# Attention on 64x64 tiles of TensorE, with the softmax sums inverted where they lie

## What is computed

```python
q, k, v = (einsum('bnd,fd->bnf', layernorm(x), W).heads(16, 64) for W in (Wq, Wk, Wv))
sim = 50 * tanh(einsum('bhid,bhjd->bhij', q, k) / 8 / 50)      # [2, 16, 1024, 1024]
attn = softmax(where(causal, sim, -max), axis=-1)
x = x + einsum('bhij,bhjd->bhid', attn, v).merge_heads() @ Wo.T
```

## Time and profile before

| | us |
|---|---|
| median of 3 runs | 1235.56 |
| lowest, highest | 1235.16, 1241.74 |
| profiled execution: time, span | 1238.81, 1237.1 |
| TensorE busy | 1153.2 |
| VectorE busy | 848.6 |
| ScalarE busy | 718.5 |
| GpSimd busy | 523.7 |

### The profile page before, as it was taken

The page is one execution under the profiler, slowest core; times in us unless marked ns, Lnnn a source line. Parts: engine busy times, 40 slices in busy tenths (PEclk is TensorE's granted clock), DMA queues, the critical chain, the costliest instruction groups (busy, mean ns, idle before and its releaser), DMA issues. The chain is left out here.

```text
span 1237.1 us, 20696 instructions
## 1 busy us (share of the span) xinstructions
PE 1153.2 (93%) x6995; PEld 575.1 (46%) x6995; DVE 848.6 (69%) x1836; ACT 718.5 (58%) x945; POOL 523.7 (42%) x545
## 2 busy tenths in 40 slices
PE   4899999999999998879997999999999999888998
PEld 1444444444444485358983222222222223446996
DVE  6456666666666555864426899999999995485441
ACT  3587787787787715512225276767767777651221
POOL 0056656656656700337863013213312311135884
PEclk9799999999999999979999999999999999897999
DMA  4000101001001110427754431322122120223765
GB/s 126 1 7 19 25 24 35 24 24 35 24 24 35 23 33 5 171 63 189 179 120 83 84 66 44 60 54 56 49 60 51 45 53 1 78 98 100 193 171 121
DMA packets 54878, 81.98 MB, mean 66 GB/s; under 512 B 18776, under 2 KB 36572, under 8 KB 53676
## 3 DMA queue, kind: packets, MB, share of 16 engines
q1 hardware_dynamic: 42728, 70.92, 21.2%
q0 software_dynamic: 10880, 8.86, 4.9%
q10 hardware_dynamic: 1192, 1.19, 0.3%
HBM read 55.38 MB, written 11.67 MB: 54 GB/s over the span
## 5 line engine op out<-in xcount | busy, mean ns | idle before, releaser
L1866 ACT ACTIVATE at_PR<-psum 128x1024 f32<-128x1024 f32 x256 | 248.0, 1021 | 121.2 <-PE psum L2098 121.0
L1934 DVE TENSOR_REDUCE at_MX<-psum 128x1 f32<-128x512 f32 x468 | 301.0, 685 | 10.0 <-PE psum L2075 5.4
L1803 POOL TENSOR_TENSOR at_PR<-at_PR,at_FAC 128x512 f32<-128x512 f32 x64 | 81.0, 1266 | 285.8 <-ACT at_PR L1866 285.8
L486 ACT ACTIVATE PR<-psum 128x1024 f32<-128x1024 f32 x144 | 141.0, 1026 | 73.7 <-PE psum L774 61.3
L774 PE MATMUL psum<-Q,K 64*128 64x512 f32 (+3 forms) x768 | 143.6, 502 | 1.1 <-ACT PR L486 1.1
L491 ACT ACTIVATE PR<-PR 128x1024 f32<-128x1024 f32 x144 | 144.6, 1062 | 0.0
L786 PE MATMUL psum<-PR,V 128*64 128x512 f32 (+3 forms) x768 | 137.4, 489 | 0.1
L2116 PE MATMUL psum<-at_PR,at_VG 128*32 128x512 f32 x1024 | 136.2, 604 | 0.0
L2098 PE MATMUL psum<-at_QS,at_KS 122*128 122x512 bf16 x512 | 133.4, 381 | 0.4 <-ACT at_PR L1866 0.2
L463 POOL TENSOR_SCALAR_AFFINE_SELECT PR<-PR 128x256 f32<-128x256 f32 (+1 forms) x112 | 58.8, 539 | 160.3 <-ACT PR L491 159.9
L1456 PE MATMUL psum<-moe_XGT,moe_WE 128*128 128x256 f32 x512 | 125.4, 390 | 0.0
(11 more groups left out here) (256 smaller groups left out, 1706.0 us busy)
## 6 DMA issues: line engine op xcount, KB each, us to landing
moe_WE<-in_c_We SPq DMA_DIRECT2D x32, 768.0 KB
XB<-at_r_dram SPq DMA_DIRECT2D x32, 256.0 KB, 3.8
at_QS<-at_SPL SPq DMA_DIRECT2D x72, 64.0 KB
at_KS<-at_SPL SPq DMA_DIRECT2D x72, 64.0 KB
at_KS<-in_c_krows SPq DMA_DIRECT2D x8, 384.0 KB
moe_rows_dram<-XNS SPq DMA_DIRECT2D x2, 1152.0 KB, 10.7
moe_spare_dram<-moe_zeros SPq DMA_DIRECT2D x2, 1024.0 KB, 13.3
moe_sum_dram<-XB SPq DMA_DIRECT2D x2, 1024.0 KB, 3.8
```

Source lines behind the costliest of these rows:

```text
L486: act.activation(PR[u][:, :, :], S[(b + u) % 2][:, :, :], ACT.Tanh, scale=SCALE0 / CLAMP).then_inc(z.clamped, 1)
L1803: pool.tensor_tensor(pr, pr, FAC[:, 4 * (s // 2):4 * (s // 2) + 4, :], ALU.mult).then_inc(z.factored, 1)
L1866: act.activation(PR[:, gu % PRS, 2 * r:2 * r + 2, :].rearrange("p h n -> p (h n)"), g.psum[:, 2 * r * BANK:(2 * r + 2) * BANK], ACT.Exp).t ...
L1934: dve.tensor_reduce(MX[:, 4 * (2 * pair + c % 2) + I % 4, khalf:khalf + 1], bank(("max", c))[:, :], AX, ALU.max).then_inc(z.reduced, 1)
```

## The change

Every matmul of the attention's loop now uses a quarter of the array, 64 rows by 64 columns.

- `scores`: each matmul is split in two column halves `c`. With the heads' row halves that makes four.
- The query blocks stand in the order `ORDER` = 2, 3, 4, 5 | 0, 1, 6, 7, one half in each output bank. A unit's first two blocks (`near`) belong to the first bank, the others (`far`) to the second.
- `multiply`: two passes. In the first, one half of the contraction (64 rows) goes to the one bank and the other half to the other bank; in the second they swap. The second pass waits for the first (`z.halved`).
- `project` for Q, K, V and `totals`: likewise in two passes over the two banks of `J`. `totals` gives 64 equal rows for each head, in both banks: its output is already broadcast.
- `copy_totals`, `spread` and `broadcast` go. `invert` takes the reciprocal of the two banks from PSUM into RB, 128x512 each, before `scale`.
- `take` moves from ScalarE to VectorE (but for the last sequence), at `n == 1` and `n == 10` in VectorE's order.
- TensorE's scores are `AHEAD` = 4 units ahead of its products. The scores of unit n + 4 stand between the two passes of unit n.
- A sequence has five masked units instead of seven, one with four diagonal blocks.

```diff
+ORDER = [2, 3, 4, 5, 0, 1, 6, 7]
+BLOCKS = [[(0, 2), (0, 3), (0, 0), (0, 1)], [(0, 4), (0, 5), (0, 6), (0, 7)], [(1, 2), (1, 3), (1, 6), (1, 7)],
+          [(2, 2), (2, 3), (2, 6), (2, 7)], [(3, 4), (3, 5), (3, 6), (3, 7)], [(3, 3), (5, 5), (1, 1), (7, 7)],
+          [(4, 4), (4, 5), (4, 6), (4, 7)], [(1, 4), (1, 5), (5, 6), (5, 7)], [(2, 4), (2, 5), (6, 6), (6, 7)]]
+PIECES = [(runs(u[0:2], 0), runs(u[2:4], 2 * P)) for u in BLOCKS]
...
+AHEAD = 4
...
@@ VectorE
-                def copy_totals(s):
+                def take(s, b, p):
+
+                    dve.wait_ge(z.multiplied, NU * s + NU)
+                    for half in range(2):
+                        dve.tensor_copy(heads_out(p, b, half * BANK, (half + 1) * BANK), O[:, half * BANK:(half + 1) * BANK]
+                                        ).then_inc(z.taken, 1)
+
+                def invert(s):
+
                     dve.wait_ge(z.totalled, s + 1)
-                    wait(dve, z.spread, 64 * s)
-                    dve.tensor_copy(DS[:, :], J[0]).then_inc(z.copied, 1)
-
-                def invert(s):
-                    dve.wait_ge(z.spread, 64 * s + 64)
-                    dve.reciprocal(RC[:, :, :], RC[:, :, :]).then_inc(z.inverted, 1)
+                    wait(dve, z.scaled, s)
+                    for j in range(2):
+                        dve.reciprocal(RB[:, j * BANK:(j + 1) * BANK], J[j]).then_inc(z.inverted, 1)
...
                 def pair(p, more):
                     first = isinstance(p, int) and p == 0
+                    for n in range(2 * NU):
+                        add_up(dve, 2 * p + n // NU, n // NU, n % NU, 0, z.summedA)
+                        if n == 1 and not first:
+                            take(2 * p - 1, 1, p - 1)
+                        if n == 10:
+                            take(2 * p, 0, p)
+                        if n in (1, 3, 5):
+                            projected(2 * p + 1, 1, n - 1)
+                            projected(2 * p + 1, 1, n)
+                        if n in (10, 12, 14) and more:
+                            projected(2 * p + 2, 0, n - 10)
+                            projected(2 * p + 2, 0, n - 9)
+                        if n == 7 and not first:
+                            invert(2 * p - 1)
+                            scale(2 * p - 1, 1, p - 1)
+                        if n == 16:
+                            invert(2 * p)
+                            scale(2 * p, 0, p)
@@ TensorE
+                def project(s, b, side, first):
+
+                    if first and side == 0:
+                        wait(pe, z.inverted, 2 * s - 4)
+                        pe.wait_ge(z.value, 2 * s)
+                    elif first:
+                        pe.wait_ge((z.query, z.key)[side - 1], 2 * s + 2)
+                    if not first:
+                        pe.wait_ge(z.part_projected, 3 * s + side - 2)
+                    passed(s)
+                    for t in range(4 if side == 2 else 1):
+                        for x in range(2):
+                            rows = row[x if first else 1 - x]
...
+                def multiply(s, b, u, swap, first):
+
+                    if first and u == 0:
                         pe.wait_ge(z.value, 2 * s + 2)
-                    if u < 2:
-                        wait(pe, z.taken, 2 * s - 1 + u)
-                    unit_done(pe, s, u)
-                    for j, at, q, w in PIECES[u]:
+                        wait(pe, z.taken, 2 * s)
+                    if first:
+                        unit_done(pe, s, u)
+                    else:
+                        pe.wait_ge(z.halved, NU * s + u + 1)
+                    passed(s)
+                    for n in range(2):
+                        for side in range(2):
+                            rows = row[side if first != swap else 1 - side]
+                            for j, at, q, w in PIECES[u][side][n:n + 1]:
+                                for h in range(2):
+                                    mm = pe.matmul(O[row[h], q:q + w], V[rows, b, j, row[h]], PR[u][rows, h, at:at + w],
+                                                   start=(first and u == 0), stop=(not first and u == NU - 1),
+                                                   skip_group_check=True)
+                    mm.then_inc(z.halved if first else z.multiplied, 1)
+
+                def totals(s, b, value, first):
+                    if first:
+                        pe.wait_ge(z.summedA, ADDED[NU] * (s + 1))
+                        pe.wait_ge(z.summedB, ADDED[NU] * (s + 1))
+                        wait(pe, z.inverted, 2 * s)
+                        pe.wait_ge(z.value, value)
+                    else:
+                        pe.wait_ge(z.part_totalled, s + 1)
+                    passed(s)
+                    for j in range(2):
+                        rows = row[j if first else 1 - j]
                         for h in range(2):
+                            mm = pe.matmul(J[j][row[h], :], g.ones[rows, 0:DH0], ACC[b][rows, h, j * BANK:(j + 1) * BANK],
+                                           start=first, stop=not first, skip_group_check=True)
+                    mm.then_inc(z.part_totalled if first else z.totalled, 1)
 
                 def pair(p, more):
...
+                    for n in range(2 * NU if more else 2 * NU - AHEAD):
+                        turned = n == 0 or n == NU and more
+                        if turned:
+                            if n:
+                                pe.wait_ge(z.w, 16 * p + 32)
+                            project(2 * p + 1 + n // NU, 1 - n // NU, 0, True)
+                            scores(*unit(n + AHEAD))
+                        multiply(*unit(n), n % 2 == 1, True)
+                        if turned:
+                            project(2 * p + 1 + n // NU, 1 - n // NU, 0, False)
+                        else:
+                            scores(*unit(n + AHEAD))
+                        multiply(*unit(n), n % 2 == 1, False)
+                        k = n % NU
+                        if 1 <= k <= 4 and (n < NU or more):
+                            project(2 * p + 1 + n // NU, 1 - n // NU, (k + 1) // 2, k % 2 == 1)
+                        if n in (5, 6) and not begin:
+                            totals(2 * p - 1, 1, 4 * p + 4, n == 5)
+                        if n in (14, 15):
+                            totals(2 * p, 0, 4 * p + 6, n == 14)
```

More of the change, by code:

```diff
@@ L389, in add_up @@
                 unit_done(eng, s, u)
-            for k, (to, w, first, second) in enumerate(ADDS[u]):
-                into = ACC[b][:, h, to:to + w]
+            for k, (n, to, first, second) in enumerate(ADDS[u]):
+                into = split(ACC[b][:, h, :], n)[:, to, :]
                 if second is None:
@@ L504, in pair @@
                             exponent(s, u)
-                        if k == 0 and not (isinstance(p, int) and p == 0):
-                            for half in range(2):
-                                take(2 * p - 1, 1, p - 1, half)
-                        if k in (4, 5):
-                            take(2 * p, 0, p, k - 4)
                 def first_copies(first, end):
@@ L790, in totals @@
-                def totals(s, b, value):
-                    pe.wait_ge(z.summedA, ADDED[NU] * (s + 1))
-                    pe.wait_ge(z.summedB, ADDED[NU] * (s + 1))
-                    pe.wait_ge(z.value, value)
-                    for h in range(2):
-                        for j in range(2):
-                            at = (2 * h + j) * ROWS
-                            mm = pe.matmul(J[0][at:at + ROWS, :], g.ones[:, 0:ROWS], ACC[b][:, h, j * BANK:(j + 1) * BANK],
-                                           start=True, stop=True, skip_group_check=True)
-                    mm.then_inc(z.totalled, 1)
@@ L881, in _ @@
                 for k in (4, 5):
-                    project(0, 0, k)
-                scores(0, 0, 0)
-                scores(0, 0, 1)
-                pe.wait_ge(f1.next.xt, 4)
+                    project_first(k)
+                for u in range(AHEAD):
+                    scores(0, 0, u)
+                    if u == 1:
+                        pe.wait_ge(f1.next.xt, 4)
                 span(pair)(pe)
-                pe.wait_ge(z.copied, last)
-                totals(last, 1, 2 * last + 2)
-                out(0, 2, PAIRS)
+                out(0, 2, PAIRS - 1)
+                totals(last, 1, 2 * last + 2, True)
+                out(0, PAIRS - 1, PAIRS)
+                totals(last, 1, 2 * last + 2, False)
                 out(1, 0, PAIRS)
                 pe.wait_ge(z.taken, 2 * last + 2)
-                pe.wait_ge(z.copied, last + 1)
+                pe.wait_ge(z.inverted, 2 * last + 2)
                 pe.wait_ge(z.added, 2)
```

203 lines of the change are left out of this document (91 added, 112 removed), and 4 rows, old and new, of the table PIECES.

## The result

The changed kernel takes **1342.83 us** (median of 4 runs, 1340.71 to 1350.41), the kernel before 1237.02 beside it (4 runs, 1235.16 to 1241.74). The ratio is 1.0848, with an interval of 1.0821 to 1.0876: 105.8 us slower. The profiled execution took 1341.23 us with a span of 1339.5, against the 1238.8 and 1237.1 on which the sum was made: 102.4 more in the profile, where the sum said 82.5. The forecast of 1318 is 25 us low. The time lies above the forecast's own range of 1300 to 1335; it lies inside the wide one of 1284 to 1350, near its upper end.

A forecast was written before the change was run, and what follows sets the result against it. TensorE was taken to bound the kernel, busy in all 46.5 us of a pair. Terms -13.5 + 80.6 + 7.3 + 1.5 + 6.6 = +82.5 us gave 1318 us against 1235.6; own range 1300 to 1335, wide range 1284 to 1350.

The forecast's parts named there:

- Quarter tiles and the start: TensorE: four 64x64 matmuls abreast at the same step, -13.5 us; more scores before the first product, +1.5 us.
- The reciprocal: VectorE: each 128x512 reciprocal out of PSUM takes 3.52 us, by a straight line through 4, 16 and 32 elements.
- rival 1: VectorE: a long reciprocal is cheap, at a copy's 0.69 us giving 1233 us, no change; chance 0.05.
- The two stops: TensorE waits 3.8 us before Q's projection and 2.4 before the first product, after 13 sequences: +80.6 us.
- The last pair: After sequence 13's sums the first product waits 7.8 us for everything; +7.3 us with the other changes there.
- The end: VectorE's chain of sums, reciprocals and scaling delays the next stage's statistics: +6.6 us.
- The granted clock: TensorE's clock during the attention: no fall counted in the sum, 0 us.
- Rival 4: TensorE's granted clock falls in the stops, 1.5 us a stop, +20 us, 1338 us; chance 0.08.
- rival 2: TensorE's instruction stream is too dense, 56 ns a MATMUL being a floor: 1377 us, or 1348 half hidden; chance 0.14.
- rival 3: Only the stop before Q's projection appears, or VectorE copies sooner: 13 x 2.4 us less, 1287 us; chance 0.08.

The follow-up runs named there:

- experiment 1: Changed kernel with VectorE copying the two banks of sums instead of taking their reciprocals, the division left out; 1233.9 us, ratio 0.9967 to the kernel before.
- experiment 2: Changed kernel with the copies of the output banks back on ScalarE, the reciprocals kept; 1301.73 us, ratio 1.0523 to the kernel before.
- experiment 6: Changed kernel with each bank's reciprocal taken twice, first into a spare buffer; 1413.47 us, ratio 1.1429 to the kernel before.

## Why the prediction was right, and what it missed

**The mechanism holds.** VectorE's reciprocals of whole rows make two stops a sequence, one of TensorE before the projection of Q, one before the first product. The timeline shows both in their places with the releasers named; experiment 1 removes both by making the instruction short, experiment 2 the second alone, experiment 6 lengthens the first by just what was added. TensorE, the bound before, isn't one any more.

**Term by term**, measured in the stage, where the kernel lost 104.9. Experiment 1 splits it: 2.7 won without the long reciprocal, 107.6 lost with it.

- *Quarter tiles and the start*, forecast -13.5 + 1.5 = -12.0, and with the tiles' share in the last pair (-0.5) and at the end (+0.9) -11.6. Four abreast cost the same step, as forecast; the pair came to 45.1 or 45.6 rather than 44.8. Measured -2.7: 8.9 too hopeful. Between sequence 0's sums and sequence 12's experiment 1 saves 5.1, where six pairs at 1.7 were to give 10.2; the rest isn't split further.
- *The reciprocal*, forecast 3.52 us, measured 3.326. The straight line through 4, 16 and 32 elements was the right idea. Its slope beyond is (3326 - 353)/480 = 6.19 ns an element, a little under the lower of the two that the rows gave, 6.3. The rate of a copy was far off. So rival 1 is out: it needed 0.77. The Trainium skill, page VectorE: DVE Perf Modes, section First, the fixed hardware budget, with the 0.96 GHz of its section Specifications, had led to an estimate of 4.27 us; the measured 3.33 is 22% below it, and measurement decides.
- *The two stops*, forecast 3.8 + 2.4 = 6.2, thirteen times 80.6. Measured 3.34 idle, and 1.5 or 2.6 in turn. A clean pair exceeds experiment 1's by 56.6 - 45.6 = 11.0, that is 5.5 a sequence, about 71.5 in all: 9.1 too much. The two reciprocals were priced 0.4 too long. VectorE's chain from the scaling to the end of the copies, put at 4.1, takes 4.3 in the one half (231.30 to 235.58) and 3.2 in the other, where the addition and the copy into the sums take 0.68 and 0.28.
- *The last pair*, one wait forecast as 7.8. It measured 6.57, and the stretch from sequence 13's sums to sequence 14's is 6.4 longer than in experiment 1: 1.4 too much.
- *The end*, forecast 6.6, 5.7 of it without the added pass of sums. From sequence 14's sums to the end of the stage the changed kernel takes 5.8 more than experiment 1. That includes a pause of TensorE of 3.0 us at 559.6 and lower clock behind it. This term was right.
- *The granted clock*, forecast 0 in the sum. **This is the step that failed.** From sequence 0's sums to sequence 13's the changed kernel takes 391.5 us and experiment 1 takes 296.3, 95.2 less. The stops are 71.5 of it, so 23.7 are left, 1.1 of them the one longer stop and some 23 the clock. Rival 4 described the fall rightly, down to nearly its size (it said 1.5 us a stop, 20 in all, 1338 us; measured 1.7 a stop), and I gave it 0.08.

Together the misses are 8.9 - 9.1 - 1.4 + 23.7 = 22.1, and 104.9 - 82.5 leaves 22.4 to explain. So the sum is short by the clock's share only because two other misses, 9 us each, cancel. That part is luck.

**Why I under-rated the clock.** My ground against it was that it stood at 1.00 through all pairs. But in those pairs TensorE never paused, so these rows say nothing of a kernel that does. What did bear on it stood on the page of before, in TensorE's own row:

```profile
PE   4899999999999998879997999999999999888998
```

Slices 1, 17, 34 and 36 are the four in which the clock row reads under 9, and in each of them TensorE reads 7 or 8. Not every slice with pauses has the lower clock (0, 15, 16, 21, 35 and 39 read 9), but no slice in which TensorE reads 9 has it. That was worth a chance nearer a half.

**The other rivals.** The instruction stream (rival 2) is no bound: scores in quarter tiles show no gap, and V's 32 MATMULs take 0.87 us, 27 ns each (L779, at 155.00 and 155.87), half of the 56 ns that were the densest before. By the Trainium skill, page TensorE: Matmul & The Clock Gate, section Wait — 56ns, not 53.3ns?, a MATMUL takes the sequencer some 62 ns when hardware decoding is off; the 27 ns of this trace exclude that here. That only the first stop appears (rival 3) is what experiment 2 had to be built for; its order on VectorE was fixed, as argued.

**What stays open.** Why one restart loses the clock and the next doesn't: the same half period came out at 27.77 three times and at 28.8 to 30.3 three times, with first stops of the same length. Why the code behind the stage, which is the same in all kernels, takes anything from 738.5 to 745.4 us. And where the quarter tiles' gain in the loop goes in the rest of the stage.

## What to carry to other kernels

An elementwise operation that looks like "the same as a copy" can cost five copies, and where its operand is a PSUM bank that the next matmul wants, all of it is TensorE's idle time: move the operation onto few elements (128x16 here: 243 ns) even if seven DMAs carry them there and back, as long as nothing waits for those DMAs. When a change makes the bounding engine stop regularly, price the stop *and* the granted clock after it: here 71 us of stops brought some 23 us of lower clock with them, and useless work in the stops gave 14 of them back. And test a moved copy for its place in the new order: the takes on ScalarE were free with stops and cost 2.8 us a pair without them.

## What the runs showed of the hardware

- A reciprocal of 128x512 fp32 out of PSUM into SBUF takes 3326 ns on VectorE, 6.2 ns an element beyond the first 32; a second one straight behind it 3295.
- Four 64x64 fp32 tiles run abreast at the step of two: eight MATMULs of 256 columns every 0.43 us, eight of 512 every 0.86, 32 of 128 every 0.87, which is 27 ns each.
- Doing more can be faster: 280 useless matmuls in the stops took 14.3 us off the time, as the granted clock stayed up.
- A lower clock and a wait can stand in for each other: with stops of 9.8 us the work after them ran at 1.2 GHz and took 1.8 us longer (3.5 instead of 1.7), and the second stop of about 2 us vanished.
- The same code takes longer from execution to execution when the granted clock ahead of it is lower: the part before the attention ended at 44.77 to 45.16 us at a mean clock of 1.00 and at 49.80 at 0.86.
